# A graph network of attention layers on one core: the end of each layer moved into the next projection, and the rest of the stage borders changed

## The chip, the core and the metric

The kernel runs on one core of a Trainium2 chip. The metric is the device time of one execution in microseconds (us); lower is better. In the profile PE is TensorE, PEld its weight loads, DVE VectorE, ACT ScalarE, POOL GpSimd and SP SyncE.

## The reference, cut to what matters

3125 nodes carry rows of 256 features, all in f32. First a graph sum over 50,000 weighted edges; then a small attention over 32,768 edges that gives the gates of four experts; then three attention layers over the 50,000 edges; at the end a routed pair of experts and a last normalisation.

```
x = x + bias + sum over edges (w * (norm(x) @ W)[target])        # the sum
x = x + sum over 4 experts (gate * expert(norm(x)))              # gates from the small attention
h = norm(x)
for l in 0, 1, 2:                                                # the attention layers
    p = h @ W_l ;  e = leaky_relu(e_src[src] + e_dst[dst], 0.2) per head
    a = exp(e - max) / (sum(exp) + 1e-16) ;  h = sum over edges (a * p[src]) + bias_l
    l = 0: h = relu(h) + norm(x)     l = 1: h = relu(h)     l = 2: x = x + relu(h + norm(x))
n = norm(x) ;  y = norm(n + 2 routed experts(n)) * gamma + beta + x
```

## The kernel before

**Stages.** The program (bottom of the file) is a list of stages; at each border all five engines wait for each other. In this order: setup; `place_edges` for the sum's edges; one long stage in which POOL scatters the edge records to eight copies of a table in DRAM (`scatter_edges`, L437, one indirect DMA for each of 400 columns) while DVE and PE normalise, project and sort the edges of both graphs (`norm_rows`, `project`, `place_fine` with the scalar_tensor_tensor of L218, `permute_edges` L403 to L421); `merge_edges`, which reads the eight copies back on SP's queue (L453) and adds them on DVE (L460 to L467); `sum_edges`; `add_sums` with the norm and the small projection; the small attention `attend_edges` with width 16; the gates; the four experts; then three times `project`, `attend_edges` with width 256 and `finish_layer`; norm; `route` (22 gathers of expert weights, L1254); two experts; the end.

**The sum.** For each of 415 columns POOL gathers 128 rows (L694), DVE makes a one-hot matrix (L645), PE multiplies (L711) and DVE adds the product to `acc` at a bucket read from memory (L651). `acc` is cleared first (L672), and `add_sums` adds it and the bias to x (L973, L975).

**The attention.** The edges are sorted into columns of 128, four columns make a step q, six steps one round of a hardware loop. For each q: POOL gathers four blocks of table rows by indirect DMA (L760) into one of six slots; ACT copies the indices (L858) and writes the penalty `pen` that masks columns of other nodes (L865, four activations 128x32); DVE subtracts it (`fence`, L779, 128x512); PE transposes (L921, four); DVE takes maxima (L808), a running maximum (L814) and small terms (L820, L825, L829), with the four accumulations of step q-2 between them (`add_up`, L794); ACT adds the destination term (`lift`, L872, four activations into `f.y`); DVE applies the leaky relu to all four columns at once (`leak`, L799, 128x512); ACT takes exponentials (`weigh`, L882, four, and L883); PE transposes back (L929), ACT copies out of PSUM (`back`, L889), PE multiplies (L937). Each engine's list is fixed: DVE does fence(q+1), maxima(q), add_up(q-2) in between, leak(q); ACT does lift(q), stage(q+6), fence(q+2), weigh(q), back(q). The leak in the kernel before:

```
y = f.y[s % 2][:, :, :]
dve.wait_ge(lifted, q + 1)
nc.vector.scalar_tensor_tensor(y, y, 0.2, y, ALU.mult, ALU.max).then_inc(leaked, 1)
```

**The end of a layer.** `finish_layer` divides the sums by the denominators (L983 to L985, one 128x6400 multiply), reorders them from (head, node) to (node, head) by 16 copies of 32x1600, seven on ACT (L1013) and nine on DVE (L1022), adds the bias (L1026) and applies relu and residual (L1028 to L1033). Then `project` loads the weights, DVE folds the attention vectors into them (L605 to L610), and for each of 25 tiles PE transposes (L574), ACT copies (L559), PE multiplies (L592, L597), DVE copies out of PSUM (L615, L616) and SP stores the rows (L545). Three PSUM banks hold products (TB = 3), so that PE can be three tiles ahead of DVE.

## Time and profile before

| what | us |
|---|---|
| median of 3 runs (4507.91 to 4516.21) | 4511.73 |
| the profiled execution | 4508.29 |
| its span | 4506.6 |
| busy of the span: PE / DVE / ACT / POOL | 2997 / 2867 / 1945 / 2488 |
| projection of layer 1, 2781 to 2841 | 60 |
| attention of layer 0, 2138 to 2748 | 610 |
| relu of layer 1, L1030, 128x6400 | 3.5 |
| last scatter issued (L437), at | 601.1 |
| scatter L437 / route's gather L1254 to landing, median | 2.2 / 2.7 |

The span runs from the first to the last instruction; the profiled execution's own time is 1.7 us longer. The median of the runs is 3.4 us above the profiled execution. No engine is busy for more than 67% of the span, so the question of what bounds the kernel has to be asked of each stage.

### The profile page before, as it was taken

To read this page: it belongs to the slowest core of one execution; us is meant where nothing else is said; L and a number is where in the kernel's file an instruction comes from. 1 tells how busy PE (TensorE), PEld (TensorE's weight loads), DVE (VectorE), ACT (ScalarE), POOL (GpSimd) and SP (SyncE) were. 2 spreads that over 40 slices of the span, in tenths; PEclk is the share of its full clock that TensorE was granted. 3 is DMA by queue.
4 is the path that set the end of the run, shared out by engine and by line. 5 is a ranking of instruction groups with operands and counts; after the bars stand their busy time and mean duration, and the time that the engine had idled before them with its cause. 6 is when DMAs were issued, how large, how long until landed. Compare 5 with 4: busy or idle time off the path is not lost. (4 is left out here: it accounts for less than half of the span.)

```text
span 4506.6 us, 87073 instructions
## 1 busy us (share of the span) xinstructions
PE 2997.2 (67%) x23551; PEld 1855.0 (41%) x23551; DVE 2867.1 (64%) x8938; ACT 1945.0 (43%) x6848; POOL 2488.0 (55%) x2504
## 2 busy tenths in 40 slices
PE   5588857776565557997666664666664676665195
PEld 3241113333243336775444443444442444443174
DVE  5779989889636562224666665566666376666525
ACT  2000000000147772112777773577775487776322
POOL 3777747777347760000777771577773477775100
PEclk8679989999655558998555556655555655555597
DMA  3000013333210000001534442544442534343000
GB/s 109 10 2 2 2 63 105 105 105 106 50 12 9 9 9 21 22 0 40 134 103 106 105 103 46 126 106 105 106 104 54 119 104 104 104 104 77 21 0 31
DMA packets 201282, 298.00 MB, mean 66 GB/s; under 512 B 110723, under 2 KB 140382, under 8 KB 201086
## 3 DMA queue, kind: packets, MB, share of 16 engines
q0 software_dynamic: 108656, 245.98, 22.1%
q1 hardware_dynamic: 92462, 50.07, 4.5%
q8 instruction: 74, 1.21, 0.1%
q14 instruction: 90, 0.74, 0.1%
HBM read 272.84 MB, written 23.05 MB: 66 GB/s over the span
## 5 line engine op out<-in xcount | busy, mean ns | idle before, releaser
L760 POOL DMA_INDIRECT work<-table_att,work x1368 | 1357.6, 992 | 1110.0 <-ACT work L858 694.0
L929 PE MATMUL psum<-ident,work 128*128 128x128 f32 x1656 | 558.8, 475 | 441.8 <-ACT work L882 439.5
L779 DVE TENSOR_TENSOR work<-work 128x512 f32<-128x512 f32 x414 | 288.2, 696 | 601.2 <-issue 288.2
L937 PE MATMUL psum<-work 128*32 128x65 f32 (+1 forms) x13248 | 417.8, 294 | 314.2 <-ACT work L889 270.9
L929 PEld LDWEIGHTS psum<-ident,work 128*128 128x128 f32 x1656 | 302.2, 182 | 741.6 <-ACT work L882 572.0
L882 ACT ACTIVATE work<-work 128x128 f32<-128x128 f32 x1656 | 529.6, 391 | 140.4 <-DVE work L799 139.6
L872 ACT ACTIVATE work<-psum,work 128x128 f32<-128x128 f32 x1656 | 472.6, 369 | 229.6 <-DVE work L808 225.0
L507 ACT ACTIVATE work<-x,stats 128x256 f32<-128x256 f32 x100 | 49.2, 493 | 1133.5 <-DVE stats L487 1133.5
L437 POOL DMA_INDIRECT sorted<-xt x400 | 414.2, 1035 | 185.5 <-issue 121.6
L937 PEld LDWEIGHTS psum<-work 128*32 128x32 f32 x13248 | 330.6, 164 | 433.9 <-issue 288.2
L794 DVE SCALAR_TENSOR_TENSOR acc<-acc,work,psum 128x65 f32 (+1 forms) x1656 | 445.5, 269 | 85.8 <-DMA acc<-table_att 15.9
L694 POOL DMA_INDIRECT work<-table_sum,index x415 | 393.4, 948 | 180.4 <-PE psum L711 97.5
L921 PE MATMUL psum<-ident,work 128*128 128x128 f32 x1656 | 461.0, 434 | 39.9 <-DVE work L779 38.7
L760 POOL DMA_INDIRECT work<-table_gate,work x288 | 300.1, 1042 | 194.6 <-ACT work L858 107.2
L711 PE MATMUL psum<-work 128*128 128x256 f32 x830 | 285.8, 434 | 180.7 <-DMA work<-table_sum,index 103.6
L865 ACT ACTIVATE work<-iota,lows 128x32 f32<-128x32 f32 x1656 | 401.8, 333 | 0.0
L921 PEld LDWEIGHTS psum<-ident,work 128*128 128x128 f32 x1656 | 295.8, 216 | 107.6 <-issue 57.1
L889 ACT COPY work<-psum 128x512 f32<-128x512 f32 x414 | 242.4, 586 | 199.3 <-PE psum L929 199.3
L1305 PE MATMUL psum<-xt,work 128*128 (+1 forms) x960 | 268.7, 439 | 73.4 <-ACTq L1344 44.3
L799 DVE SCALAR_TENSOR_TENSOR work<-work 128x512 f32<-128x512 f32 x414 | 285.5, 690 | 19.6 <-ACT work L872 19.4
L808 DVE TENSOR_REDUCE work<-psum 128x512 f32 (+1 forms) x414 | 285.8, 690 | 2.3
L421 PE MATMUL psum<-work 128*128 128x504 f16 x800 | 240.4, 384 | 44.7 <-DVE work L405 2.5
(302 smaller groups left out, 4265.7 us busy)
## 6 DMA issues: line engine op xcount, KB each, us to landing
work<-table_att,work POOLq DMA_INDIRECT x1368
table_att<-acc SPq DMA_DIRECT2D x75, 132.0 KB
acc<-table_att SPq DMA_DIRECT2D x12, 812.5 KB, 18.5
work<-table_sum,index POOLq DMA_INDIRECT x415, 2.7
sorted<-xt POOLq DMA_INDIRECT x400, 2.2
sorted<-work SPq DMA_DIRECT2D x8, 622.5 KB, 8.0
work<-sorted SPq DMA_DIRECT2D x8, 622.5 KB, 7.6
work<-table_gate,work POOLq DMA_INDIRECT x288, 2.5
```

What stands on the lines that cost most here:

```text
L437: nc.gpsimd.indirect_dma_start(out=rec_dram[s], out_offset=bass.IndirectOffsetOnAxis(ap=row[:, f:f + 1], axis=0), in_=record[:, f, :], in_ ...
L694: nc.gpsimd.indirect_dma_start(out=f.rows[c % RS][:, :], out_offset=None, in_=table, in_offset=bass.IndirectOffsetOnAxis(ap=index[:, c:c + ...
L711: nc.tensor.matmul(ps[c % PS], f.hot[c % PS][:, :], f.rows[c % RS][:, :], start=True, stop=True).then_inc(summed, 1)
L760: nc.gpsimd.indirect_dma_start(out=rows[s][:, t, :], out_offset=None, in_=table[:, 0:rw], in_offset=bass.IndirectOffsetOnAxis(ap=f.index[s ...
L779: nc.vector.tensor_tensor(f.z[s % 2], rows[s][:, :, hw:rw].unsqueeze(3).to_broadcast([P, QD, HEADS, DB]), f.pen[s % 2][:, :, :].unsqueeze( ...
L794: nc.vector.scalar_tensor_tensor(acc[:, b, :], acc[:, b, :], f.fac[s][:, t:t + 1], ps_s[s % 2][:, t, :], ALU.mult, ALU.add).then_inc(taken, 1)
L865: ins = nc.scalar.activation(f.pen[s % 2][:, t, :], m.iota[:, 0:DB], ACT.Square, scale=STEP, bias=lows[:, bass.ds(q * QD + t, 1)])
L872: ins = nc.scalar.activation(f.y[s % 2][:, t, :], ps_z[s % 2][:, t * P:(t + 1) * P], ACT.Identity, bias=dst[:, bass.ds(q * QD + t, 1)])
L882: nc.scalar.activation(f.pt[s % 2][:, t, :], f.y[s % 2][:, t, :], ACT.Exp, bias=f.neg[s][:, t, 1:2]).then_inc(exped, 1)
L921: ins = nc.tensor.transpose(ps_z[s % 2][:, t * P:(t + 1) * P], f.z[s % 2][:, t, :, :].rearrange("p h d -> p (h d)"), m.ident[:, :])
L929: nc.tensor.transpose(ps_p[s % 2][:, t * P:(t + 1) * P], f.pt[s % 2][:, t, :], m.ident[:, :]).then_inc(turned2, 1)
L937: ins = nc.tensor.matmul(ps_s[s % 2][DB * h:DB * (h + 1), t, :], f.p[s % 2][:, t, DB * h:DB * (h + 1)], rows[s][:, t, h * w1:(h + 1) * w1] ...
```

## The change

- **Attention.** `pen` moves from SBUF to PSUM banks 6 and 7, so L779 subtracts a PSUM operand, and ACT's first penalties wait for `ready` (the banks hold two start values before). `lift` now writes 0.2 * (z + dst) to `f.y` (scale 0.2 and a new `fifth_dst`), and `leak` is four instructions of 128x128 that compute max(z + dst, f.y) with z in PSUM; PE's next transposes into that bank wait for `leaked` and no longer for `lifted`.
- **End of layers 0 and 1.** `finish_layer` is left for the last layer alone. In `project` DVE does `settle(g)` for groups of five tiles: division, ten copies of 32x320 (POOL does the other six), for layer 0 relu and residual; for layer 1 the relu is in ACT's copy of the transposes. The order on DVE: settle(0), fold, settle(1), then for each group its five takes and settle(g+2).
- **Bias.** It is added to the projected rows (the copy L615 becomes an add), since the weights of a node's edges sum to one; the bias adds of 128x6400 go away.
- **The sum.** It adds straight to x, after one add of the bias; the clear of `acc` and `add_sums` go away. Buckets are held to 24.
- **Merge.** Four copies in place of eight; their reads are on SP's queue in the long stage, behind `ranked` (both sorts done) and the scatter's semaphores, and DVE's adds follow the permutation in the same stage.
- **Route.** POOL no longer waits for the 22 gathers to land; the experts wait for theirs.

```diff
-COPIES = 8
+COPIES = 4
-        chain.next(nc.vector.tensor_copy(bucket, ps_bucket))
+        chain.next(nc.vector.tensor_scalar(bucket, ps_bucket, float(NT - 1), None, ALU.min))
...
     @block.sync
+        sp.wait_ge(ranked, 1)
         for k in range(COPIES):
+            sp.wait_ge(m.scatter_sent[k], 16 * (columns_for(edges) // COPIES))
             sp.dma_start(parts[:, k, :], rec_dram[k][0:P * ncol, :].rearrange("(p c) k -> p (c k)", p=P)).then_inc(back, 16)
...
     @block.scalar
+            if prior == 1:
+                nc.scalar.activation(turned_tile(t), ps_t[t % TB], ACT.Relu).then_inc(copied, 1)
...
+    if prior is not None:
+        @block.gpsimd
+        def _(pool):
+            for g in range(NT // GN):
+                pool.wait_ge(scaled, g + 1)
+                for out, part in places(g)[:POOLED]:
+                    ins = nc.gpsimd.tensor_copy(out, part)
+                ins.then_inc(moved, 1)
+        def settle(g):
+            of, tiles = slice(4 * GN * g, 4 * GN * (g + 1)), slice(GN * g, GN * (g + 1))
+            den = m.den[:, :, :].rearrange("p t h -> p (t h)")[:, of]
+            chain.next(nc.vector.tensor_scalar(den, sums[:, of, dh], 1e-16, None, ALU.add))
+            chain.next(nc.vector.reciprocal(den, den))
+            nc.vector.tensor_tensor(sums[:, of, 0:dh], sums[:, of, 0:dh], den.unsqueeze(2).to_broadcast([P, 4 * GN, dh]), ALU.mult).then_inc(scaled, 1)
+            dve.wait_ge(scaled, g + 1)
+            for out, part in places(g)[POOLED:]:
+                ins = nc.vector.tensor_copy(out, part)
+            chain.next(ins)
+            dve.wait_ge(moved, g + 1)
+            if prior == 0:
+                nc.vector.scalar_tensor_tensor(src[:, tiles, :], src[:, tiles, :], 0.0, m.xn[:, tiles, :], ALU.max, ALU.add).then_inc(after, 1)
+            else:
+                dve.sem_inc(after, 1)
...
+            settle(0)
+            fold()
+            settle(1)
+            for g in range(NT // GN):
+                ones_for(slice(GN * g, GN * (g + 1)))
+                for t in range(GN * g, GN * (g + 1)):
+                    take(t)
+                if g + 2 < NT // GN:
+                    settle(g + 2)
...
-            nc.vector.tensor_tensor(m.acc[:, b, 0:D], m.acc[:, b, 0:D], ps[c % PS], ALU.add).then_inc(taken, 1)
+            nc.vector.tensor_tensor(m.x[:, b, :], m.x[:, b, :], ps[c % PS], ALU.add).then_inc(taken, 1)
...
-        nc.vector.memset(m.acc[:, :, :], 0.0).then_inc(cleared, 1)
         for c in range(PS):
             mark(c)
+        dve.wait_ge(loaded, 16)
+        nc.vector.tensor_tensor(m.x[:, :, :], m.x[:, :, :], m.bias[:, :].unsqueeze(1).to_broadcast([P, NT, D]), ALU.add).then_inc(biased, 1)
...
+    ps_pen = [m.psum[6 + s][:, 0:QD * DB].rearrange("p (t d) -> p t d", t=QD) for s in range(2)]
...
             nc.vector.tensor_tensor(f.z[s % 2], rows[s][:, :, hw:rw].unsqueeze(3).to_broadcast([P, QD, HEADS, DB]),
-                                    f.pen[s % 2][:, :, :].unsqueeze(2).to_broadcast([P, QD, HEADS, DB]), ALU.subtract).then_inc(masked, 1)
+                                    ps_pen[s % 2].unsqueeze(2).to_broadcast([P, QD, HEADS, DB]), ALU.subtract).then_inc(masked, 1)
...
         def leak(q, s):
-            y = f.y[s % 2][:, :, :]
             dve.wait_ge(lifted, q + 1)
-            nc.vector.scalar_tensor_tensor(y, y, 0.2, y, ALU.mult, ALU.max).then_inc(leaked, 1)
+            for t in range(QD):
+                fifth = f.y[s % 2][:, t, :]
+                ins = nc.vector.scalar_tensor_tensor(fifth, ps_z[s % 2][:, t * P:(t + 1) * P], dst[:, bass.ds(q * QD + t, 1)], fifth, ALU.add, ALU.max)
+            ins.then_inc(leaked, 1)
...
+        nc.vector.tensor_scalar(fifth_dst, ps_dst, 0.2, None, ALU.mult).then_inc(ready, 1)
...
-                ins = nc.scalar.activation(f.pen[s % 2][:, t, :], m.iota[:, 0:DB], ACT.Square, scale=STEP, bias=lows[:, bass.ds(q * QD + t, 1)])
+                ins = nc.scalar.activation(ps_pen[s % 2][:, t, :], m.iota[:, 0:DB], ACT.Square, scale=STEP, bias=lows[:, bass.ds(q * QD + t, 1)])
...
-                pe.wait_ge(lifted, q + (-1))
+                pe.wait_ge(leaked, q + (-1))
...
-        pool.wait_ge(got, 2 * 11 * 16)
...
+            pe.wait_ge(m.expert_got[0], 11 * 16)
```

## Rows read from the trace of the kernel before

**Rows 1.** Windows: stretch, busy of PE, PEld, DVE, ACT, POOL, clock, DMA share, GB/s.

```profile
2138.00:2748.00 610.00, 401.21 (x4564) 263.11 (x4564) 401.23 (x1257) 456.53 (x1704) 451.05 (x456) 0.50 0.44 107
2781.00:2841.00 60.00, 48.24 (x250) 31.87 (x250) 15.90 (x59) 12.46 (x39) 0.00 (x0) 0.90 0.21 68
```

**Rows 2.** Groups of POOL: count, busy us, mean ns, idle before by releaser.

```profile
L760 POOL DMA_INDIRECT work<-table_att,work x1368 | 1357.6, 992 | 1110.0 <-ACT work L858 694.0 <-issue 402.3 <-PE psum L937 13.7
...
L760 POOL DMA_INDIRECT work<-table_gate,work x288 | 300.1, 1042 | 194.6 <-ACT work L858 107.2 <-issue 80.5 <-PE psum L937 7.0
```

**Rows 3.** Line L760: what POOL sat idle for, us and times; ns min/median/max.

```profile
L760 POOL DMA_INDIRECT work<-table_att,work x1368: 940/946/1479, 2138.3 to 4137.5; - x196
...
  ACT work L858: 801.2, 4
```

**Rows 4.** Timeline of one step of the small attention, POOL and DVE.

```profile
1401.68 0.69 DVE L779 TENSOR_TENSOR work<-work 128x512 f32<-128x512 f32 x1 [2.29 <-DMA work<-table_gate,work]
1401.76 1.43 POOL L760 DMA_INDIRECT work<-table_gate,work  x1 [0.30 <-issue]
...
1404.62 0.68 DVE L799 SCALAR_TENSOR_TENSOR work<-work 128x512 f32<-128x512 f32 x1
1404.74 1.38 POOL L760 DMA_INDIRECT work<-table_gate,work  x1 [0.30 <-issue]
```

**Rows 5.** Windows of L437 alone: POOL busy, beside L218, then beside L403 to L405.

```profile
200.00:340.00 140.00, 106.64 (x110) 0.67 0.03 4
344.00:600.00 256.00, 200.84 (x182) 0.99 0.02 2
```

**Rows 6.** Groups by form, 130 to 345: L218 adds a PSUM and an SBUF tile.

```profile
L218 DVE SCALAR_TENSOR_TENSOR xt<-psum,xn,xt 128x400 f32<-128x400 f32 x100 | 58.3, 632 | 7.6 <-PE psum L170 7.4
L218 DVE SCALAR_TENSOR_TENSOR xt<-psum,xn,xt 128x256 f32<-128x256 f32 x100 | 39.5, 476 | 0.1
```

**Rows 7.** Timeline of DVE: start, us; twelve of L218 in a row.

```profile
51.74 6.83 DVE L218 SCALAR_TENSOR_TENSOR xt<-psum,xt 128x400 f32<-128x400 f32 x12 [0.27 <-PE psum L170]
```

**Rows 8.** Timeline: the last full step of layer 0's attention.

```profile
2739.31 0.59 ACT L889 COPY work<-psum 128x512 f32<-128x512 f32 x1 [0.47 <-PE psum L929]
...
2741.67 1.56 DVE L794 SCALAR_TENSOR_TENSOR acc<-acc,work,psum 128x65 f32 x4
...
2743.62 0.59 ACT L889 COPY work<-psum 128x512 f32<-128x512 f32 x1 [0.47 <-PE psum L929]
```

**Rows 9.** Timeline from the end of layer 0's attention to layer 1's last tile.

```profile
2747.93 0.25 DVE L983 TENSOR_SCALAR den<-acc 128x100 f32<-128x100 f32 x1 [0.34 <-PEq L1561]
...
2756.00 9.27 DVE L1022 COPY xt<-acc 32x1600 f32<-32x1600 f32 x9
...
2785.55 0.69 DVE L608 TENSOR_TENSOR prod<-work,att 128x512 f32<-128x512 f32 x1 [4.17 <-DMA att<-in_L_gnn_ad_dram]
...
2830.82 0.42 DVE L615 COPY acc<-psum 128x256 f32<-128x256 f32 x1 [1.33 <-PE psum L597]
...
2836.20 0.15 DVE L616 COPY acc<-psum 128x4 f32<-128x4 f32 x1
```

**Rows 10.** Timeline of setup: POOL's widest operation that is no DMA.

```profile
1.39 0.54 POOL L87 IOTA work<- 128x504 int32 x1
```

**Rows 11.** Timeline: merge after the permutation, and the sum's first gather.

```profile
644.38 5.55 DVE L460 TENSOR_TENSOR work<-work 128x1245 f32<-128x1245 f32 x4 [15.37 <-DMA work<-sorted]
...
656.47 0.98 POOL L694 DMA_INDIRECT work<-table_sum,index  x1 [54.29 <-SPq L1561]
```

**Rows 12.** Timeline: add_sums, start of the norm.

```profile
1184.69 6.82 DVE L973 TENSOR_TENSOR x<-x,acc 128x6400 f32<-128x6400 f32 x1 [0.32 <-PEq L1561]
...
1198.63 1.49 DVE L486 TENSOR_REDUCE stats<-x 128x5 f32<-128x1280 f32 x1 [0.25 <-DVE x L975]
```

**Rows 13.** Timeline: last gather of the route, first weights and matmul of the experts.

```profile
4275.66 0.95 POOL L1254 DMA_INDIRECT work<-in_L_ffn_b_dram,expert_rows  x1 [0.30 <-issue]
4281.68 0.50 PEld L1305 LDWEIGHTS psum<-xt,work 128*128 128x128 f32 x2 [44.36 <-ACTq L1344]
```

More of the change, by code:

```diff
@@ L425, in scatter_edges @@
 def scatter_edges(nc, block, m, name, edges, rec_dram, record, row):
-    sent = [m.dma_sem(f"{name}_sent{s}") for s in range(COPIES)]
+    sent = m.scatter_sent
     fc = columns_for(edges)
@@ L510, in _, with project @@
             nc.scalar.activation(std[:, at], var[:, at], ACT.Sqrt, scale=1.0 / D, bias=m.eps[:, 0:1]).then_inc(squared, 1)
-def project(nc, block, m, name, w_in, width, src, table, att_src=None, att_dst=None, at_dram=None, keep_t=None, after=None):
+def project(nc, block, m, name, w_in, width, src, table, att_src=None, att_dst=None, at_dram=None, keep_t=None, after=None, bias_in=None, prior=None):
     att = att_src is not None
@@ L610, in _, with take @@
             nc.vector.tensor_copy(wt[:, :, width:n_w], wa[:, :, 0:HEADS]).then_inc(folded, 1)
-        for t in range(NT):
+        def take(t):
             dve.wait_ge(made, t + 1)
-            if att:
-                heads = rows[:, t, 0:hw].rearrange("p (h w) -> p h w", h=HEADS)
-                nc.vector.tensor_copy(heads[:, :, 0:dh], ps_h[t % TB][:, 0:width].rearrange("p (h c) -> p h c", h=HEADS))
-                nc.vector.tensor_copy(rows[:, t, hw:rw], ps_h[t % TB][:, width:n_w]).then_inc(taken, 1)
-            else:
-                nc.vector.tensor_copy(rows[:, t, 0:width], ps_h[t % TB]).then_inc(taken, 1)
@@ L621, in sum_edges @@
-def sum_edges(nc, block, m, name, table, rec, index, bucket, edges, nch, record, lows, sources):
-    hot, summed, taken, cleared, built, moved, steps = (m.sem(f"{name}_{s}") for s in ("hot", "summed", "taken", "cleared", "built", "moved", "steps"))
+            if not att:
+                nc.vector.tensor_copy(rows[:, t, 0:width], ps_h[t % TB]).then_inc(taken, 1)
+                return
+            heads = rows[:, t, 0:hw].rearrange("p (h w) -> p h w", h=HEADS)
+            made_h = ps_h[t % TB][:, 0:width].rearrange("p (h c) -> p h c", h=HEADS)
@@ new lines, in take, with ones_for @@
+            if bias_in is None:
+                nc.vector.tensor_copy(heads[:, :, 0:dh], made_h)
+            else:
+                nc.vector.tensor_tensor(heads[:, :, 0:dh], made_h, m.bias[:, :].rearrange("p (h c) -> p h c", h=HEADS), ALU.add)
+            nc.vector.tensor_copy(rows[:, t, hw:rw], ps_h[t % TB][:, width:n_w]).then_inc(taken, 1)
+        def ones_for(tiles):
+            nc.vector.memset(rows[:, tiles, 0:hw].rearrange("p t (h w) -> p t h w", h=HEADS)[:, :, :, dh], 1.0)
+        if prior is None:
+            if att:
+                ones_for(slice(0, NT))
+                fold()
+            for t in range(NT):
+                take(t)
+        else:
+            settle(0)
+            fold()
+            settle(1)
+            for g in range(NT // GN):
+                ones_for(slice(GN * g, GN * (g + 1)))
+                for t in range(GN * g, GN * (g + 1)):
+                    take(t)
+                if g + 2 < NT // GN:
+                    settle(g + 2)
@@ L625, in sum_edges @@
+def sum_edges(nc, block, m, name, table, rec, index, bucket, bias_in, edges, nch, record, lows, sources):
+    hot, summed, taken, biased, built, moved, steps, loaded = (m.sem(f"{name}_{s}") for s in ("hot", "summed", "taken", "biased", "built", "moved", "steps", "loaded"))
     fc = columns_for(edges)
```

112 lines of the change are left out of this document (56 added, 56 removed).

## The prediction

> **What bounds the kernel now.** I read it stage by stage. The windows show that a layer's attention takes about 610 us and its projection 60 [rows 1]. With the small attention the four stages of this kind are half of the span, so their bound comes first. In the attention no engine looks full: ACT 457 of 610, POOL 451, PE and DVE 401 [rows 1]. The groups of POOL settle it: a gather of a layer is 992 ns and the idle time before it that ends by itself ("issue") is 402.3 / 1368 = 0.30 us, so one every 1.29 us; in the small attention 1042 ns [rows 2]. POOL waited for ACT only four times in all, once at the start of each attention [rows 3]. So POOL is in its own list all the time: four gathers make a step of 5.17 us in the layers and 5.37 in the small attention. That pace is the bound. The steps are 1368 / 4 = 342 and 288 / 4 = 72, and they take 342 x 5.17 + 72 x 5.37 = 2155 us.
>
> The gathers don't all take the same: minimum 940, median 946 ns, maximum 1479 [rows 3]. The timeline shows what makes the long ones: a gather that starts 0.08 us after L779 takes 1.43 us, one that starts 0.12 us after L799 takes 1.38 [rows 4]; each ends 0.82 us after the end of its DVE instruction, as if it had begun there. Both DVE instructions read two tiles of SBUF.
>
> **Attention: the gain.** After the change neither of them reads two SBUF tiles: L779 takes its penalty from PSUM, the leak takes z from PSUM. Would such a form still hold POOL up? L218 has exactly the leak's form, a PSUM tile and an SBUF tile; beside it POOL's scatters take 106.64 / 110 = 0.97 us, against 200.84 / 182 = 1.10 beside DVE's one-input 16-bit copies at L403 to L405 [rows 5]. So I take the delays as gone: 1368 x (992 - 945) + 288 x (1042 - 945) = 64 + 28 = 92 us. The other end is 0, if the second input is not what delays.
>
> **Attention: the price.** The step then has 4 x (0.945 + 0.30) = 4.98 us, and the next limit must stay below it. It is the ring lift, leak, weigh, PE's transposes, back, lift; where no gather is waited for, at the end of the stage, it turns in 2743.62 - 2739.31 = 4.31 us [rows 8], with a leak of 0.69. The new leak is four instructions. L218's two widths, 632 ns for 400 columns and 476 for 256 [rows 6], give 1.08 ns per column and so 337 ns for 128. Twelve of them in a row take 6.83 us, (6.83 - 0.63) / 11 = 0.56 from start to start, 0.07 less than each lasts [rows 7]. Leak: 3 x 0.27 + 0.34 = 1.14 us, ring 4.31 + 0.45 = 4.76: under 4.98. The other end of this price is L794, which computes a register's address and waits for the one before: four in 1.56 us at 280 ns each, 0.15 over their length [rows 8]; so priced the leak is 3 x 0.49 + 0.34 = 1.80 and the ring 5.42. I take 1.14, since the leak's four pieces don't wait for each other, as L218's don't. PE's next transposes wait for the leak in place of the lift, but they stand behind the transposes back of the same step, which need the leak anyway: nothing. ACT's first penalties wait for `ready`, and DVE makes `fifth_dst` first (504 columns, at most the 0.7 of L799): both are covered by POOL, which has six steps of gathers to issue before it needs the first sum. At the end of a stage the last steps run at the ring's pace, +0.45 for one or two of them, and start less late than now. I set these against a gain of 92 and take 90.
>
> A rule speaks against splitting the leak. The Trainium skill (VectorE: DVE Perf Modes, "The TRN2 errata — SBUF-src ops pay a fixed extra latency per instruction") says that a fixed cost is paid by each instruction, and gives 120 + columns cycles at 0.96 GHz for a PSUM source. An estimate by that figure is 4 x 248 / 0.96 = 1.03 us for the leak. By it the ring would be 4.65, also under the gathers; the rows' own price is higher and is the one used.
>
> **End of layers 0 and 1.** Now: from the first division to the last take of layer 1 is 2836.35 - 2747.93 = 88.4 us [rows 9]; layer 1's own end has the relu L1030 of 3.5 us (in the table above) in place of 6.8, so 85. After: a group's division is a fifth of 6.8 (a multiply of 1280 columns, 1.5 us with its start-up) and 0.4 for the small ones; DVE's ten copies of 32x320 cost a fifth of the columns of L1022 (9.27 / 9 = 1.03 us [rows 9]) and the same start-up, 0.2 by L218 (476 - 256 x 1.08 [rows 6]): 0.36 each, 3.6 us; POOL's six copies have no row; its iota of 504 columns takes 0.54 us [rows 10], so 320 columns some 0.4, 2.4 us in all; relu and residual 1.5. Side by side with POOL a group of layer 0 is 7.0 us, one after the other 9.4 (layer 1: 5.5 and 7.9). The rows show delays between DVE and POOL but never a full exclusion of such copies; I take 9.4 and 7.9, because DVE's copies are, like L403 to L405, of one input in SBUF, the kind that delayed the scatters [rows 5], and keep the other end for the range. Fold: four of 0.69 and a small one, 2.9 [rows 9]. A tile on PE is 48.24 / 25 = 1.9 us [rows 1], and PE can be three tiles ahead, so behind each settle two tiles are waited for: with the takes 0.42 [rows 9] and 0.15, 4.3 us. Layer 0: 9.4 + 2.9 + 9.4 + 3 x (4.3 + 9.4) + 4.3 + 5 x 1.9 = 76.6 us, gain 12; layer 1: 7.9 + 2.9 + 7.9 + 3 x 12.2 + 13.8 = 69, gain 16. Side by side they would be 64.6 and 57: 24 and 28. Against this stands PE's clock: it is 0.50 through the whole attention, and 0.90 in the present projection, which PE fills [rows 1]. With PE idle some 3 us behind each settle it may fall back to 1.2 GHz between groups; I take 4 us a layer for that. Sum: 20 us for both.
>
> The Trainium skill (SBUF — State Buffer, "Who interferes with whom") says that a DVE instruction in a two-port mode and a GpSimd instruction exclude each other fully. By it the copies of a group come one after the other, which is the 9.4 us taken, and the sum stays; no row here has such a pair.
>
> **Last layer.** Its end keeps its form but loses the bias add of 128x6400: 6.8, as L973 [rows 12]. SP's bias loads move to before the table stores and land under the first settle: nothing. The bias in the takes makes a copy an add of the same width: nothing.
>
> **Merge.** Now the permutation ends at 644.38 - 15.37 = 629.0 and the sum's first gather is at 656.5 [rows 11]. The four reads stand on SP's queue behind the scatter, whose last DMA is issued at 601 (table above); eight of them kept DVE waiting for 15.4 us, four take some 8, to 611: the permutation covers them. Of seven big adds (5.55 / 4 = 1.39 us each) three are left: from the first add to the first gather it is 656.5 - 644.4 = 12.1 us now and 12.1 - 5.6 = 6.5 then, so the sum starts at 635.5, gain 21. With four copies a scatter waits for the fourth before it, at least 4 x 1.27 = 5.1 us back [rows 5] against a landing of 2.2 in the median: nothing; if it did wait, there are 28 us of slack.
>
> **Sum.** The clear goes and an add of 6.8 us comes, beside POOL's gathers, which run 16 ahead (20 us) and set the pace: nothing. add_sums: 1198.63 - 1184.69 = 13.9 us [rows 12].
>
> **Route.** The last gather ends at 4276.6, the experts' first weights load at 4281.7 [rows 13], and a median landing is 2.7 of it (table above). POOL must still issue all 22 before the border. Gain 2.7.
>
> **Sum of it:** 90 + 20 + 6.8 + 21 + 13.9 + 2.7 = 154 us off the profiled execution's 4508.3, 4354; the median of the runs is 3.4 above it, so 4357.
>
> **Rivals.** (A) The ring takes over: the leak's pieces each carry a register's address and cost what L794's do. Place: DVE between lift and weigh; price: leak 1.80, ring 5.42 us, 414 x 5.42 = 2244 against 2155 now, 89 lost where 90 were won; from a leak of 1.36 us on the ring is above 4.98, and from 1.74 us on (ring 5.36) it costs more than the 64 us that the other parts bring. All in all 4508.3 - 64 + 89 + 3.4 = 4537: slower. For it: the pieces have addresses from a register, as L794's. Against: ACT's lift has the same addressing and its four overlap. Chance 6%; a ring between 4.98 and 5.3 another 8%, 4357 to 4425. (B) The change doesn't do what it says at POOL: the delays stay, 4357 + 90 = 4447. Against it stand the scatters beside L218 [rows 5]. 5%. (C) PE stays at 1.2 GHz in the two projections: a tile takes nearly double, 3.6 us, 25 of them 90 us behind 12 of settle and fold, 102 and 101 in place of 88 and 85: 30 lost where 20 were won, 4407. For it: 0.50 at 401 of 610 us busy [rows 1]. 10%.
>
> **Numbers.** My case, 70%: 4357, itself 4325 (24 less without exclusion of the copies, some 6 less for earlier ends of the attentions) to 4385. The range 4325 to 4425 takes in C and most of the middling ring and leaves B and A out. A measurement of this kernel can tell about 0.2%, 9 us. Faster 0.93, same 0.01, slower 0.06.
>
> **What would show it.** L760 at about 945 ns in all four attentions; steps of 4.98 us; the ring's leak at about 1.14 us with POOL still not waiting for L858 or L937; the sum's first gather near 636; no gap between the sum and the norm; projections of layers 1 and 2 near 77 and 69 us from the first division to the last take, with the clock mostly 1.00. I am wrong if gathers stay near 992, if POOL waits for ACT or PE in the loop, or if the clock in the projections is 0.50.

## The result, and the profile after

The changed kernel takes 4345.5 us (median of 4 runs, 4342.0 to 4348.6), the kernel before 4510.8 in the same comparison: a ratio of 0.9632, 95% interval 0.9615 to 0.9649. The forecast was 4357, range 4325 to 4425, faster. The rows here are from the profiled execution of 4348.6 us, span 4346.8, against 4506.6 before. Of all executions in this document two, one of the kernel called border below and one of the first joined kernel, ran at a lower granted clock (0.60 and 0.62 where the others have 0.67 to 0.69), and no time or ratio here uses them.

The same cuts in both traces account for the whole difference:

| stretch | before, us | after, us | change | forecast |
|---|---|---|---|---|
| start to the sum's first gather | 656.5 | 636.3 | -20.2 | -21 |
| sum, from there to the next stage's first instruction | 528.2 | 535.4 | +7.2 | 0 |
| add_sums | 13.9 | 0 | -13.9 | -13.9 |
| four attentions, first to last gather | 2161.2 | 2070.6 | -90.6 | -90 |
| last gather of layer 0 to first of layer 1 | 113.7 | 99.6 | -14.1 | -8 |
| last gather of layer 1 to first of layer 2 | 112.8 | 88.7 | -24.1 | -12 |
| last gather of layer 2 to the end | 368.1 | 362.4 | -5.7 | -9.5 |
| gates and first experts; norm and gate projection | 552.1 | 553.9 | +1.8 | 0 |

**Attention.** The groups of POOL and the waits of the whole span, after; they answer to [rows 2, 3]:

```profile
L831 POOL DMA_INDIRECT work<-table_att,work x1368 | 1293.7, 946 | 929.7 <-ACT work L932 513.0 <-issue 376.6 <-PE psum L1011 40.1
L831 POOL DMA_INDIRECT work<-table_gate,work x288 | 271.8, 944 | 181.8 <-ACT work L932 94.3 <-issue 78.0 <-PE psum L1011 9.4
...
POOL work L831 <- ACT work L932: 607.3, 7, 469.3
...
POOL work L831 <- PE psum L1011: 49.6, 157, 2.0
```

A gather's mean is 946 and 944 ns where it was 992 and 1042, which is the old median. POOL waited for ACT 7 times in all stages together, and for PE's sum 157 times, all but one for 0.3 us: one gather after the other is still what sets the pace. The timeline of a step, after, answers to [rows 4]. Columns: start, us, engine, line; in brackets how long the engine had sat idle, and what ended that:

```profile
2199.78 0.68 DVE L850 TENSOR_TENSOR work<-work,psum 128x512 f32<-128x512 f32 x1
2199.79 0.94 POOL L831 DMA_INDIRECT work<-table_att,work  x1 [0.30 <-issue]
...
2203.49 1.13 DVE L871 SCALAR_TENSOR_TENSOR work<-psum,work 128x128 f32<-128x128 f32 x4 [0.61 <-ACT work L946]
2203.54 0.95 POOL L831 DMA_INDIRECT work<-table_att,work  x1 [0.30 <-issue]
```

The same pairs that stood 0.08 and 0.12 us apart before, with gathers of 1.43 and 1.38, now have gathers of 0.94 and 0.95. The leak's four pieces last 1.13 us together, the forecast's 1.14.

**Merge and sum.** The timeline of DVE from the end of the permutation, after; it answers to [rows 11, 12]:

```profile
628.88 0.67 DVE L413 SCALAR_TENSOR_TENSOR sources<-work,psum 128x504 int32<-128x504 int32 x1
629.78 1.46 DVE L461 TENSOR_TENSOR work<-work 128x1245 f32<-128x1245 f32 x1 [0.24 <-DVE sources L413]
...
634.67 0.43 DVE L467 TENSOR_SCALAR rec<-rec 128x415 f32<-128x415 f32 x1
635.63 1.76 DVE L714 TENSOR_SCALAR work<-iota,rec 128x128 f32<-128x128 f32 x6 [0.53 <-PEq L1614]
638.60 6.82 DVE L744 TENSOR_TENSOR x<-x,bias 128x6400 f32<-128x6400 f32 x1 [1.22 <-DMA bias<-in_L_gnn_bias_dram]
```

And the timeline of POOL beside it:

```profile
636.29 1.05 POOL L764 DMA_INDIRECT work<-table_sum,index  x1 [33.50 <-SPq L1614]
637.64 0.96 POOL L764 DMA_INDIRECT work<-table_sum,index  x1 [0.30 <-issue]
638.90 7.34 POOL L764 DMA_INDIRECT work<-table_sum,index  x1 [0.30 <-issue]
```

The reads are there when DVE comes to them. But the third gather lasts 7.34 us: it starts 0.30 us after the add of x and bias, which reads two SBUF tiles, and ends at 646.24, 0.82 us after the add's end at 645.42. That is the distance of the delayed gathers of [rows 4], in a place where the forecast said "nothing".

**Ends of the layers.** DVE's timeline of layer 0's end, then POOL's beside it, after; they answer to [rows 9]:

```profile
2675.20 0.18 DVE L631 TENSOR_SCALAR den<-acc 128x20 f32<-128x20 f32 x1 [0.34 <-PEq L1614]
2675.41 0.28 DVE L632 RECIPROCAL den<-den 128x20 f32<-128x20 f32 x1
2675.73 1.49 DVE L633 TENSOR_TENSOR acc<-acc,den 128x1280 f32<-128x1280 f32 x1
2677.25 4.34 DVE L636 COPY xt<-acc 32x320 f32<-32x320 f32 x10
2681.63 1.49 DVE L640 SCALAR_TENSOR_TENSOR xt<-xt,xn 128x1280 f32<-128x1280 f32 x1
```

```profile
2677.28 2.99 POOL L621 COPY xt<-acc 32x320 f32<-32x320 f32 x6 [22.66 <-DVE acc L633]
```

A settle takes 7.8 us, from its first division to the next instruction. The copies of DVE (4.34) and POOL (2.99) start together and run side by side. From the first division to the last take the two projections last 73.7 and 62.6 us. Windows of layer 1's projection (PE, PEld, DVE, ACT, POOL busy, then the granted clock):

```profile
2674.00:2686.00 12.00, 1.11 (x4) 0.71 (x4) 10.98 (x22) 0.74 (x2) 2.79 (x6) 0.50 0.24 55
2686.00:2700.00 14.00, 13.78 (x64) 8.59 (x65) 11.35 (x29) 2.59 (x7) 2.80 (x6) 0.83 0.15 50
2700.00:2714.00 14.00, 10.97 (x52) 6.94 (x51) 9.83 (x26) 1.84 (x5) 2.80 (x6) 0.88 0.14 49
...
2740.00:2750.00 10.00, 8.41 (x44) 5.21 (x42) 2.75 (x13) 1.80 (x5) 0.00 (x0) 1.00 0.21 74
```

Once layer 1's tiles run, the clock moves between its two levels: 0.88 is a mean of 0.50 and 1.00. The timeline of PE at the same place in the two projections (layer 1, then layer 2), and the windows just behind, show when it falls:

```profile
2706.42 0.41 PE L589 MATMUL psum<-ident,xt 128*128 128x128 f32 x2 [3.03 <-DVE xt L640]
3374.36 0.41 PE L589 MATMUL psum<-ident,xt 128*128 128x128 f32 x2 [1.58 <-DVEq L642]
```

```profile
2708.00:2711.00 3.00, 3.00 (x10) 1.70 (x10) 0.49 (x2) 0.37 (x1) 0.00 (x0) 0.50 0.39 136
3374.00:3380.00 6.00, 5.64 (x32) 3.91 (x32) 3.67 (x15) 0.77 (x2) 0.00 (x0) 1.00 0.34 113
```

In layer 1 PE sat idle for 3.03 us behind each of the last three settles, and each time, a little after it had started again, the clock was 0.50 for some 3 us. In layer 2, whose settle is shorter, the three gaps are 1.6 us and the clock stays at 1.00. DVE then waits for a group's last two tiles for 3.9 us in layer 1 and for 2.0 in layer 2: the fall of the clock costs about 1.9 us a group there.

**The tail.** The last layer's end fell from 40.0 to 33.2 us, the 6.8 of the bias add. The last gather of the route now starts at 4116.73 and the experts' first weights load at 4121.79, 5.06 us instead of the 6.02 of [rows 13]: 1.0 gained. Against it, the last attention's end, from its last gather to the first division, grew from 19.2 to 21.3 us.

### The profile page after: what moved, and what is told of

It is laid out like the page before. It is cut to its first block and busy times, and to the rows that moved or that the text cites. A ratio compares the mean times of both kernels' runs of the same rounds, so it can differ in the third digit from the quotient of the medians.

```text
span 4346.8 us, 89648 instructions
## 1 busy us (share of the span) xinstructions
PE 3011.2 (69%) x23551; PEld 1857.9 (43%) x23551; DVE 3038.2 (70%) x10292; ACT 1892.8 (44%) x6834; POOL 2429.8 (56%) x2564
## 5 line engine op out<-in xcount | busy, mean ns | idle before, releaser
L831 POOL DMA_INDIRECT work<-table_att,work x1368 | 1293.7, 946 | 929.7 <-ACT work L932 513.0
L871 DVE SCALAR_TENSOR_TENSOR work<-psum,work 128x128 f32<-128x128 f32 x1656 | 465.0, 343 | 77.0 <-ACT work L946 71.9
L437 POOL DMA_INDIRECT sorted<-xt x400 | 413.8, 1035 | 186.1 <-issue 121.3
L1011 PEld LDWEIGHTS psum<-work 128*32 128x32 f32 x13248 | 331.9, 165 | 433.9 <-DVE acc L865 363.7
L865 DVE SCALAR_TENSOR_TENSOR acc<-acc,work,psum 128x65 f32 (+1 forms) x1656 | 445.1, 269 | 80.5 <-DMA acc<-table_att 15.8
L850 DVE TENSOR_TENSOR work<-work,psum 128x512 f32<-128x512 f32 x414 | 283.7, 685 | 273.0 <-issue 158.1
L939 ACT ACTIVATE psum<-iota,lows 128x32 f32<-128x32 f32 x1656 | 393.4, 311 | 30.9 <-DVE work L912 30.9
L831 POOL DMA_INDIRECT work<-table_gate,work x288 | 271.8, 944 | 181.8 <-ACT work L932 94.3
```

The lines of the kernel that those rows point to most:

```text
L437: nc.gpsimd.indirect_dma_start(out=rec_dram[s], out_offset=bass.IndirectOffsetOnAxis(ap=row[:, f:f + 1], axis=0), in_=record[:, f, :], in_ ...
L831: nc.gpsimd.indirect_dma_start(out=rows[s][:, t, :], out_offset=None, in_=table[:, 0:rw], in_offset=bass.IndirectOffsetOnAxis(ap=f.index[s ...
L865: nc.vector.scalar_tensor_tensor(acc[:, b, :], acc[:, b, :], f.fac[s][:, t:t + 1], ps_s[s % 2][:, t, :], ALU.mult, ALU.add).then_inc(taken, 1)
L871: ins = nc.vector.scalar_tensor_tensor(fifth, ps_z[s % 2][:, t * P:(t + 1) * P], dst[:, bass.ds(q * QD + t, 1)], fifth, ALU.add, ALU.max)
L939: ins = nc.scalar.activation(ps_pen[s % 2][:, t, :], m.iota[:, 0:DB], ACT.Square, scale=STEP, bias=lows[:, bass.ds(q * QD + t, 1)])
L1011: ins = nc.tensor.matmul(ps_s[s % 2][DB * h:DB * (h + 1), t, :], f.p[s % 2][:, t, DB * h:DB * (h + 1)], rows[s][:, t, h * w1:(h + 1) * w1] ...
```

## The experiments

Twelve kernels, each the changed kernel with one edit, except the first, which takes back three, and the last two, which join two and three. Ratios are against the kernel before on the same chip; the changed kernel's own is 0.9632. One thing has to be known to read them: all but the one with the border do the same as the changed kernel up to the sum, and yet the sum's first gather came between 626.9 and 644.9 us. A single span therefore moves by some us, and I compare stages within the profiled executions, with the ratios beside them. That the sum starts 20.2 us earlier is such a single span too.

**Which of the two delays was it?** Three kernels: all three edits of the attention back, the penalty alone, the leak alone.

```diff
-                                    ps_pen[s % 2].unsqueeze(2)...
+                                    f.pen[s % 2][:, :, :].unsqueeze(2)...
```

```diff
-            for t in range(QD):
-                fifth = f.y[s % 2][:, t, :]
-                ins = nc.vector.scalar_tensor_tensor(fifth, ps_z[s % 2][:, t * P:(t + 1) * P], dst[...], fifth, ALU.add, ALU.max)
-            ins.then_inc(leaked, 1)
+            y = f.y[s % 2][:, :, :]
+            nc.vector.scalar_tensor_tensor(y, y, 0.2, y, ALU.mult, ALU.max).then_inc(leaked, 1)
```

> The changed kernel with the attention's three edits taken back: penalty in SBUF, lift unscaled, leak as one instruction of 128x512 on two SBUF tiles. If POOL's delays are the whole of the attention's gain, 4345 + 91 = 4436 us, gathers of the layers back from 0.946 to about 0.99 us. If the other parts had won part of what the four attention stages show (an earlier start of something, another spacing), it stays below 4420. If the gain was larger than the stages show, above 4450.

> The changed kernel with the penalty alone back in SBUF, so that the fence L850 reads two SBUF tiles again, once a step. By the spacings of before, some 33 of the 91 us belong to the fence: 4345 + 33 = 4378, and the gathers' mean near 0.963. Rival: an SBUF penalty delays nothing and the leak was the whole cause: 4345. Other rival: the two delays share one cost, so that either alone brings back all 91: 4436.

> The changed kernel with the leak alone as before (one instruction of 128x512, both inputs the same SBUF tile). By the spacings of before some 57 us belong to it: 4345 + 57 = 4402. With the penalty's 33 it should make 90, the sum that both bring back together. Rivals: 4345 (only the fence delays) or 4436 (either alone brings all back).

Measured: ratios 0.9849 (0.9832 to 0.9865), 0.9693 (0.9677 to 0.9709) and 0.9721 (0.9705 to 0.9738); 4450.4, 4380.1 and 4390.4 us, where 4436, 4378 and 4402 were expected. The groups of POOL in each, in that order:

```profile
L831 POOL DMA_INDIRECT work<-table_att,work x1368 | 1361.7, 995 | 927.9 <-ACT work L930 510.7 <-issue 401.2 <-PE psum L1009 16.0
L831 POOL DMA_INDIRECT work<-table_gate,work x288 | 315.6, 1096 | 181.8 <-ACT work L930 94.3 <-issue 84.1 <-PE psum L1009 3.4
```

```profile
L831 POOL DMA_INDIRECT work<-table_att,work x1368 | 1310.1, 958 | 929.8 <-ACT work L932 512.9 <-issue 374.6 <-PE psum L1011 42.3
L831 POOL DMA_INDIRECT work<-table_gate,work x288 | 292.3, 1015 | 181.9 <-ACT work L932 94.4 <-issue 83.5 <-PE psum L1011 4.0
```

```profile
L831 POOL DMA_INDIRECT work<-table_att,work x1368 | 1339.2, 979 | 928.4 <-ACT work L930 512.1 <-issue 402.7 <-PE psum L1009 13.6
L831 POOL DMA_INDIRECT work<-table_gate,work x288 | 276.2, 959 | 181.8 <-ACT work L930 94.3 <-issue 83.5 <-PE psum L1009 4.0
```

The spans from first to last gather, small attention and the three layers together, in us:

| kernel | small attention | three layers | over the changed kernel |
|---|---|---|---|
| changed | 359.3 | 1711.3 | |
| penalty in SBUF | 379.7 | 1727.4 | +36.5 |
| leak on SBUF | 363.7 | 1755.8 | +48.9 |
| both | 403.1 | 1778.9 | +111.4 |
| before | 387.6 | 1773.6 | +90.6 |

Each brings a part of the delays back and both together bring all. The traces show which gathers are long. In the changed kernel none of the 1656 is over 1.00 us. In the others every gather over 1.00 us starts while one of the two instructions with two SBUF inputs runs, and its median end is 0.82 us behind that instruction's end:

| kernel | small attention: long gathers, us over 0.945 in all | three layers |
|---|---|---|
| penalty in SBUF | 49, 20.5 | 53, 16.7 |
| leak on SBUF | 13, 4.4 | 180, 45.1 |
| both | 107, 43.6 | 236, 67.5 |
| before | 70, 28.2 | 231, 63.7 |

These sums are the differences of the spans to within 1.5 us, so the delayed gathers are all of it. For the penalty only the place of the operand changes, so its second SBUF input is the cause. For the leak one instruction on SBUF also takes the place of four with PSUM; that one instruction of 128x512 is not too long by itself is shown by L850, which has the same width and, with its penalty in PSUM, holds no gather. In the layers the parts nearly add up (16.1 + 44.5 = 60.6 against 67.6). In the small attention they don't, 20.4 + 4.4 against 43.8, because the number of gathers that happen to start inside one of the instructions doesn't add up either: 49 and 13 apart, 107 together, and 70 in the kernel before, which has the same two instructions. That number depends on where in the step they fall, which the other waits set; what shifts it between these kernels I can't say. A total of 111 is not the gain of 90.6, and the expectation "above 4450 if the gain was larger than the stages show" was badly put for that reason.

**How much room has the ring?**

```diff
+            for t in range(QD):
+                ins = nc.vector.scalar_tensor_tensor(f.again[s % 2][:, t, :], ps_z[s % 2][:, t * P:(t + 1) * P], dst[...],
+                                                     f.y[s % 2][:, t, :], ALU.add, ALU.max)
             for t in range(QD):
```

> The leak's four instructions issued twice, the first four into a tile of their own that nobody reads: 1.12 us more of DVE in each step, on the ring lift, leak, weigh, transposes back. The prediction's ring of 4.76 us becomes 5.88 and passes the gathers' 5.00: 414 steps x 0.88 = 364 us more, 4710. If the ring has more slack than that, less: with a ring of 4.3 us now, 5.42 and 174 us more, 4519. If the leak is not on the ring, 4345 and nothing but DVE's busy time grows.

Measured: 4684.6 us, ratio 1.0367 (1.035 to 1.0385). The timeline of DVE in the middle of layer 0's attention:

```profile
2402.03 1.12 DVE L870 SCALAR_TENSOR_TENSOR work<-psum,work 128x128 f32<-128x128 f32 x4 [0.66 <-ACT work L949]
2403.07 1.12 DVE L874 SCALAR_TENSOR_TENSOR work<-psum,work 128x128 f32<-128x128 f32 x4
...
2407.88 1.13 DVE L870 SCALAR_TENSOR_TENSOR work<-psum,work 128x128 f32<-128x128 f32 x4 [0.68 <-ACT work L949]
...
2413.67 1.13 DVE L870 SCALAR_TENSOR_TENSOR work<-psum,work 128x128 f32<-128x128 f32 x4 [0.60 <-ACT work L949]
```

DVE waits for the lift (L949) and the next first piece comes 5.79 us later. The four more pieces cost 2403.07 - 2402.03 = 1.04, so the ring of the changed kernel turns in 4.75 us (forecast 4.76). By the ratios the kernel is (1.0367 - 0.9632) x 4511 = 331 us slower than the changed one, and 414 x (5.79 - 5.00) = 327 of them are there. The ring is a closed second limit, 0.25 us per step below the gathers. The expected 4710 took 1.12 for the four more pieces, which overlap. Four pieces at 0.26 from start to start don't wait for each other. Rival A's leak of 1.80 would have made the ring 4.75 + 0.67 = 5.42 and cost 414 x 0.42 = 174 us, about half of what this kernel shows (an estimate from these numbers).

**The gather of 7.34 us.** ACT copies the bias row to PSUM and DVE adds from there:

```diff
-        for c in range(PS):
+        for c in range(PS - 1):
             mark(c)
-        dve.wait_ge(loaded, 16)
-        nc.vector.tensor_tensor(m.x[:, :, :], m.x[:, :, :], m.bias[:, :].unsqueeze(1)...
+        dve.wait_ge(spread, 1)
+        nc.vector.tensor_tensor(m.x[:, :, :], m.x[:, :, :], ps_bias.unsqueeze(1)...
         dve.wait_ge(biased, 1)
+        mark(PS - 1)
...
+        nc.scalar.copy(ps_bias, m.bias[:, :]).then_inc(spread, 1)
```

> In the sum's stage ACT copies the loaded bias row into an unused half of a PSUM bank, and DVE's add x + bias of 128x6400 reads it from there; one matmul tile's mark is made after it, so that PE stays out of that bank. If the gather of 7.34 us was held by the add's two SBUF inputs, no gather of the stage is over 1.5 us now, the stage from the first gather to the norm falls from 535.4 us to 529, and the whole to 4339. Rival: the length of the add is what matters, whatever it reads: the gather of 7.3 us stays, 4345. Other rival: the gather is free but the stage's end is set by DVE's or PE's backlog from the start: 535 all the same.

Measured: ratio 0.9642 (0.9623 to 0.966), no different from 0.9632; 6 us are less than it can tell. The stage tells it: 529.4 us from the first gather to the norm where it was 535.4. Timeline, POOL and DVE:

```profile
637.85 0.95 POOL L771 DMA_INDIRECT work<-table_sum,index  x1 [0.30 <-issue]
638.11 6.82 DVE L750 TENSOR_TENSOR x<-x,psum 128x6400 f32<-128x6400 f32 x1 [2.16 <-ACT psum L709]
639.10 0.95 POOL L771 DMA_INDIRECT work<-table_sum,index  x1 [0.30 <-issue]
640.35 0.94 POOL L771 DMA_INDIRECT work<-table_sum,index  x1 [0.30 <-issue]
```

An add of the same 6.82 us and the same 6400 columns, its second input in PSUM: no gather beside it is longer than 0.95. It is the input, not the length. In the ten profiled executions with this add on SBUF there is one such gather each, of 6.5 to 7.6 us; in the three with its input in PSUM there is none. The stage is shorter by 6.0 us, as expected.

**Do DVE's and POOL's copies exclude each other?**

```diff
-    POOLED = 6
+    POOLED = 0
```

> DVE makes all 16 copies of a group, POOL none. If POOL's copies slow DVE's beside them, each DVE copy falls from 0.43 us to the prediction's 0.36, the copies of a group take 5.8 us in place of 4.35, and with 5 groups in two layers, of which all but the little that PE covers is paid, the kernel is 10 to 15 us slower: 4355 to 4360. If 0.43 is simply what a copy takes, they take 6.9, 2.5 more for each of 10 groups: 4370. If the copies excluded each other fully in the changed kernel, 16 by DVE alone would be no slower than 10 and 6: 4345.

Measured: ratio 0.9699 (0.9676 to 0.9723); the projections take 85.1 and 74.0 us, 11.4 each more, so 2.3 a settle. The tile xt in this kernel, and then in the changed one (min/median/max ns):

```profile
L634 DVE COPY xt<-acc x160: 345/351/356, 2677.3 to 3416.6; 32x320 f32<-32x320 f32 x160
```

```profile
L636 DVE COPY xt<-acc x100: 351/456/482, 2677.3 to 3395.6; 32x320 f32<-32x320 f32 x100
L621 POOL COPY xt<-acc x60: 441/447/569, 2677.3 to 3394.2; 32x320 f32<-32x320 f32 x60
```

A DVE copy alone is 351 ns, the forecast's 0.36, and 456 beside one of POOL's. Neither end of the forecast holds: one after the other the group's copies would take 10 x 0.351 + 6 x 0.447 = 6.2 us, side by side without harm 3.5, measured 4.3. The 16 copies take 5.8 us by DVE alone, as the first branch of the expectation had it, against 4.3: 1.5 for each of ten settles, 15 us. The projections lost 22.8, and that the whole came out at the second branch's 4370 (4370.7) is chance. The other 8 us are longer waits of DVE for PE, and the clock again. In layer 2 PE now sits idle for 3.05 us behind each of the last three settles where it was 1.6, the clock falls to 0.50 behind each gap, and DVE waits 3.6 us for a group's last two tiles in place of 2.0; in layer 1 the gaps grew from 3.03 to 4.49 us and the waits by 4.1 us in all.

The Trainium skill (SBUF — State Buffer, "Who interferes with whom") says that a DVE instruction in a two-port mode and a GpSimd instruction fully block each other. The copies do look like that mode: 1600 columns take 1.03 us [rows 9] and 320 take 0.351, so (1.03 - 0.351) / 1280 = 0.53 ns a column where L218 needs 1.08. Yet a copy of DVE loses 30% beside one of POOL's and not its whole length; the measured 4.3 us decides. The same section holds, marked as inferred, that a tensor_tensor on two SBUF tiles takes only the shared read interface and leaves the generation of a DMA's descriptors alone, and, without that mark, that a DVE instruction with two SBUF inputs contends with a GpSimd instruction that reads SBUF. For an indirect gather, whose row numbers lie in SBUF, the second statement fits the 7.34 us beside L744; no run here separates its reads from its descriptors.

**Is it PE's clock?**

```diff
+        if prior is not None:
+            warm(30)
         turn(0)
         turn(1)
+        if prior is not None:
+            warm(8)
```

> In the projections of layers 1 and 2, PE does 30 matmuls of 128 columns on the identity into a bank not yet in use while it waits for the first settle, and 8 more while it waits for the fold. If the clock is 0.50 at the start because PE had been idle, the first tile's transposes and matmuls run at 1.00 and the first group shrinks by some 3 us a layer: 4339. If the pace of the first tiles is set by DVE anyway, 4345. If the 30 matmuls are still running when the settle is done, some 2 us a layer slower: 4349.

Measured: ratio 0.9643 (0.9624 to 0.9662); the projections take 73.7 and 62.0 us, against 73.7 and 62.6. The clock did change, in windows of the same kind:

```profile
2684.00:2695.00 11.00, 10.89 (x74) 10.93 (x75) 10.49 (x20) 0.65 (x2) 2.78 (x6) 0.74 0.20 61
2695.00:2709.00 14.00, 12.41 (x73) 8.41 (x72) 11.35 (x29) 2.59 (x7) 2.80 (x6) 1.00 0.15 50
2709.00:2723.00 14.00, 10.97 (x53) 6.91 (x52) 9.83 (x26) 1.85 (x5) 2.80 (x6) 0.88 0.14 49
```

The first group ran at 1.00 in place of 0.83 and nothing came of it in layer 1 (0.6 us in layer 2): PE is three tiles ahead there and waits for DVE's second settle in any case. A clock that is raised under a wait is worth nothing. The kernel leaves the later gaps as they are, so it says nothing of the fall behind them. In its profile the last scatter was issued at 629.1 in place of 601.7, and DVE's way from the end of the permutation to the sum's first gather took 20.2 us where it is 6.7 in the changed kernel and in the ten others with this stage unchanged. The forecast gave the four reads 28 us of slack behind the last scatter; in one profiled execution of twelve it was used up.

**Who waits for whom in a group?** The takes of a group's last three tiles between the instructions of the next settle, where DVE used to wait for PE first:

```diff
-        def settle(g):
+        def settle(g, between=()):
...
+            if takes:
+                take(takes.pop(0))
             dve.wait_ge(scaled, g + 1)
-            for out, part in places(g)[POOLED:]:
+            for n, (out, part) in enumerate(places(g)[POOLED:]):
                 ins = nc.vector.tensor_copy(out, part)
+                if n % 3 == 2 and takes:
+                    take(takes.pop(0))
...
-                    settle(g + 2)
+                    settle(g + 2, range(GN * (g + 1) - 3, GN * (g + 1)))
```

> The last three takes of a group are issued between the instructions of the settle of the group two further on (one behind the multiply, two between the copies), so that DVE doesn't wait for PE ahead of each settle. A group costs DVE 7.8 + 5 x 0.55 = 10.6 us where it costs 12.3 to 14 now; three such groups in each of two layers: 10 to 18 us less, 4327 to 4335. If PE is what bounds, since its tiles take 1.9 us at full clock and more at 0.50, it is 4340 to 4345; if PE's clock falls in between, no gain.

Measured: ratio 0.961 (0.959 to 0.963), projections 61.4 and 58.5 us, 12.3 and 4.1 less. Windows of layer 1's projection here:

```profile
2689.00:2701.00 12.00, 11.88 (x56) 7.48 (x55) 11.64 (x28) 2.40 (x7) 4.98 (x11) 0.85 0.10 36
2701.00:2713.00 12.00, 11.51 (x64) 7.65 (x63) 11.60 (x32) 2.57 (x7) 3.24 (x8) 1.00 0.20 68
2713.00:2725.00 12.00, 11.46 (x62) 7.28 (x60) 11.62 (x29) 2.96 (x9) 2.71 (x6) 1.00 0.20 69
```

DVE and PE are both busy for 11.5 of 12 us where the changed kernel had 9.8 and 11.0 of 14. PE's three gaps of 3.03 us are down to 0.5, and the clock stays at 1.00 from the second window on. So the order of the takes, DVE waiting for PE's last two tiles and PE then for the settle, was what the projection of layer 1 still lost, and it lost it twice: by the wait itself and by the clock that fell behind it. Of the 12.3 us some 6 are the clock's, an estimate from the 1.9 us a group above. In layer 2 PE has no gap left behind its first tiles; its 25 tiles (about 1.83 us each, 46 in all) behind the first settle and the fold (9.5) are nearly the whole of the 58.5.

**The overlap, and the border.** First the ends of layers 0 and 1 as stages of their own, then the merge in its own stage with four copies:

```diff
-                        ...bias_in=a["L1_gnn_" + b], prior=k - 1 if k else None)
+                        ...bias_in=a["L1_gnn_" + b])
...
+            with Stage(nc, m) as block:
+                finish_layer(nc, block, m, f"finish{k}", k)
```

> The ends of layers 0 and 1 again as stages of their own ahead of the projections, all of the layer at once, without the bias add (it stays in the projected rows). From the last gather of a layer to the first of the next the kernel before took 113.7 and 112.8 us, the changed one 99.6 and 88.7. If the bias add is worth its 6.8 us and the rest is the overlap, this kernel takes 106.9 and 106.0: 7 and 17, together 24 to 25 us slower than the changed one, 4370. If the overlap brought nothing and all of the gain was the add and the smaller multiply, 4345 to 4350.

```diff
+        with Stage(nc, m) as block:
...
             merge_edges(nc, block, m, "merge", E, sorted_dram, m.rec[:, :], m.index[:, :], ranked)
```

> Still four copies, but the merge in a stage of its own behind the permutation, so its four reads start at the border. From the end of the permutation's last DVE instruction to the sum's first gather it was 27.5 us before and is 6.7 now. By the prediction's numbers (some 8 us for four reads, the same three adds) it is 15 us here, 8 to 9 more: 4354. If it is 6 to 8 us, the four copies alone had brought nearly all; if it stays over 20, the reads' time doesn't go with their number and the place in the long stage did it.

Measured: 0.9708 (0.9693 to 0.9723) and 0.9665 (0.965 to 0.9679). Apart, the gaps between the gathers are 109.3 and 106.7 us in place of 99.6 and 88.7: the overlap is worth 9.7 + 18.0 = 27.7 of the 38.2 that the two ends gained, the bias adds and the rest 10.5. This kernel also has the layer's copies on ACT and DVE again and layer 1's relu on DVE, so "the overlap" here is all of that together. With the border, the merge waits again (timeline):

```profile
643.49 1.46 DVE L461 TENSOR_TENSOR work<-work 128x1245 f32<-128x1245 f32 x1 [9.30 <-DMA work<-sorted]
```

From the end of the permutation to the first gather it is 15.8 us, against 27.5 before and 6.7 after (expected 15). The halved copies are worth 11.7 of the 20.8, the place 9.1: four reads at the border keep DVE waiting for 9.3 us where eight kept it for 15.4.

**Together.** The PSUM bias and the takes between, and then with 8 copies of a group for POOL:

```diff
-    POOLED = 6
+    POOLED = 8
```

> Both edits that shortened their stages together: the sum's bias add from PSUM (6 us off its stage) and the takes between the settle's instructions (12 and 4 us off the two projections). They touch different stages, so 22 us below the changed kernel: 4323. If one covers the other, less.

> The same with POOLED 8 in place of 6: DVE's eight copies at 0.456 us make 3.6, POOL's eight at 0.466 make 3.7, so a settle is 0.7 us shorter. Where DVE sets the pace of the projection that is up to 7 us in all, 4316 to 4320; where PE's 25 tiles do, which hide all but the first two settles, 3 us: 4320. If POOL starts its copies later than DVE or takes longer beside it, 4323 to 4328.

Measured: 4322.0 us, ratio 0.9585 (0.957 to 0.96), and 4319.3, ratio 0.9586 (0.9572 to 0.9601). Both lie below the changed kernel's 0.9632. The two edits add up: sum 529.2, projections 61.4 and 57.8. With 8 copies for POOL they are 59.1 and 57.1 us, 3.0 less together, and the two ratios can't be told apart. So some 0.5% was still to be had in the two places that the forecast passed over.

## Why the prediction was right, and where it wasn't

Forecast 4357, measured 4345.5, 11.5 less, in the range and on the side given 0.93. Of these, 5 are in the profiled executions (154 forecast, 160 measured); the rest is that the median lay 3.1 us below the profiled execution where the forecast put it 3.4 above. And the 5 hide misses that cancel for the most part: the ends of layers 0 and 1 brought 18.2 more than forecast, the sum cost 7.2, the tail 3.8 and the stages between 1.8 that the forecast didn't have. So the mechanisms were right for the attention and the merge, and that the total is so close is in part luck.

- **"So I take the delays as gone"**: right. Gathers 945 forecast, 946 and 944 measured, 90.6 us where 90 were taken. That a PSUM input doesn't delay was inferred from other lines; the three kernels with SBUF inputs back, and the count of long gathers in each, show it for these.
- **Leak 1.14, ring 4.76**: measured 1.13 and 4.75. Rival A needed a leak over 1.36 to count (1.38 by the measured ring); the doubled leak shows that this limit is real: 1.04 us more of leak, 0.25 of it covered, cost 331 us.
- **Layer ends, "I take 9.4 and 7.9"**: a mis-sized term, on the careful side. The settle takes 7.8 us and in layer 2 6.6 (its first division starts at 3346.63, the fold at 3353.19), since DVE's and POOL's copies overlap at a price of 30% instead of going one after the other. Five settles at 1.6 and five at 1.3 are 14.5 us. The base of layer 2 was low too: the forecast made it 85 by subtracting the relu, and the kernel before takes 87.0 there.
- **"I take 4 us a layer for that" (PE's clock)**: right for layer 1, in mechanism and nearly in size, and nothing for layer 2. The low clock at the start costs next to nothing, as the warmed kernel shows. Settles at 7.8 and 6.6 in the forecast's own sum give 76.6 - 8 = 68.6 and 69 - 6.5 = 62.5; measured 73.7 and 62.6, so 5.1 and 0.1 over it. The three falls of the clock behind gaps of 3.03 us, 1.9 us each, cover the 5.1; behind the gaps of 1.6 in layer 2 it doesn't fall. The kernel without POOL's copies, whose gaps in layer 2 are 3.05 us, shows the fall there as well. In total the two ends gained 38.2 where 20 were forecast.
- **Sum, "beside POOL's gathers ... nothing"**: wrong, 7.2 us, of which 6.0 went with the input moved to PSUM. It was the very mechanism that I had priced for the attention: the new L744 reads x and bias, both in SBUF, while POOL gathers. I counted the 20 us that gathers run ahead and didn't ask what the add does to a gather itself.
- **Merge 21**: 20.2. The nearness is luck, since the start of the sum moves by up to 18 us from kernel to kernel, but the part that belongs to the merge doesn't: from the end of the permutation to the first gather 27.5 before and 6.7 after, 20.8 less, and 15.8 with the border where 15 was expected.
- **Route, 2.7**: 1.0. The whole landing was written off; 5.06 us still lie between the last gather's start and the first weights. What they are made of wasn't tried.
- **"+0.45 for one or two" steps at the attentions' ends**: 0.6, 0.2 and 2.1 us in the three layers; the last is 1 to 2 more than taken.
- **Rivals**: B is excluded by the gathers' mean, A by the leak and the ring above, C by clocks of 0.83 to 1.00 in the windows while the tiles run, though its mechanism is there for some 3 us in three groups of layer 1.

## What to carry to other kernels

When a mechanism has been found in one stage, go through every instruction that the change adds and ask the same of it: here two edits removed a second SBUF input from beside POOL's gathers and a third put one in. Where a chain of small steps sits just under another limit, measure its slack by doubling one step, which gives the ring to a few hundredths of a microsecond. Beside POOL's gathers, count how many of them start inside such an instruction: the count and the lengths gave each difference of the spans, also where two edits didn't add up. And where two engines hand tiles back and forth, look first at which of the two waits at the group's edge. Warming the clock ahead of a wait won nothing; moving three takes closed PE's gaps, kept the clock up with them, and won 16 us.

## What the hardware showed that I had not expected

- One DVE add of 6.82 us with two SBUF inputs held a single gather for 7.34 us, to 0.82 us behind the add's end; the same add with one input in PSUM held none. In the attentions a gather that started inside a DVE instruction of 0.7 us with two SBUF inputs ended 0.82 us behind it as well.
- DVE copies of 32x320 go from 351 to 456 ns beside POOL's copies, which take 447: a price of 30%, neither none nor all.
- The cost of the delays is not additive in the small attention (20.4 and 4.4 us alone, 43.8 together), since the number of gathers that start inside one of the instructions isn't (49 and 13 alone, 107 together). What sets that number is open.
- In layer 1's projection the granted clock fell from 1.00 to 0.50, for some 3 us, behind each of PE's three idle gaps of 3.03 us, and in layer 2's it stayed at 1.00 behind three gaps of 1.6 us. Each fall cost DVE 1.9 us of waiting.
